# Who forms the low halves of the expert weights in two routing stages: VectorE around each pair of row tiles, in place of GpSimd

## What is computed

```python
x = L0_attn_hidden_states
x = x + 0.5 * _L0_ffn_ref(_layernorm(x), W_gate, b_gate, W_e, b_e)
x = x + _L0_attn_ref(_layernorm(x), Wqkv, q_ln_w, q_ln_b, k_ln_w, k_ln_b, Wout)
x = x + 0.5 * _L0_ffn_ref(_layernorm(x), W_gate, b_gate, W_e, b_e)

def _L0_ffn_ref(x, W_gate, b_gate, W_e, b_e):
    logits = x @ W_gate + b_gate
    _, top_idx = jax.lax.top_k(logits, 2)
    y_all = relu(einsum('bsd,edh->bseh', x, W_e) + b_e)
    return take_along_axis(y_all, top_idx[..., None], axis=2).mean(axis=2)
```

## Time and profile before

| | before |
|---|---|
| median of 3 runs (range) | 1069.3 us (1067.76 to 1070.01) |
| profiled execution: its time, its span | 1067.34 us, 1065.6 us |
| busy: PE, DVE, ACT, POOL | 876.0, 670.0, 443.9, 355.4 us |
| routing 1, up to its last list of tokens | 0 to about 105 us of the span |
| routing 2 | about 784 to 912 us of the span |

### The profile page before, as it was taken

One profiled execution on the slowest core, in us unless ns is written; L12 is line 12 of the kernel. 1 busy time (PEld: TensorE's weight loads), 2 busy tenths in 40 slices (PEclk: granted clock), 3 DMA queues, 4 the chain that ended last, 5 costly groups with the idle time before them and its releaser, 6 DMA issues. The chain is left out here.

```text
span 1065.6 us, 20204 instructions
## 1 busy us (share of the span) xinstructions
PE 876.0 (82%) x6688; PEld 640.8 (60%) x6689; DVE 670.0 (63%) x1295; ACT 443.9 (42%) x817; POOL 355.4 (33%) x340
## 2 busy tenths in 40 slices
PE   3676799993699987838999999999959984699994
PEld 3564688872477776725555555555437863488873
DVE  7977244431788988837777777777527676344431
ACT  3332233331134433334777777777723430133331
POOL 5540677764012321220000000000014440477764
PEclk9997799997799999977999999999979895699997
DMA  8873578863226488664666666554047882378773
GB/s 262 284 261 119 163 143 150 149 120 62 46 85 188 149 217 203 164 201 119 146 147 136 135 138 138 132 137 119 25 134 245 291 277 99 75 141 158 145 134 49
DMA packets 123099, 162.08 MB, mean 152 GB/s; under 512 B 16864, under 2 KB 74336, under 8 KB 122752
## 3 DMA queue, kind: packets, MB, share of 16 engines
q1 hardware_dynamic: 105168, 123.85, 41.5%
q0 software_dynamic: 17856, 37.25, 18.8%
HBM read 97.44 MB, written 67.37 MB: 155 GB/s over the span
## 5 line engine op out<-in xcount | busy, mean ns | idle before, releaser
L825 DVE TENSOR_REDUCE att_part<-att_s_ps 128x2 f32<-128x1024 f32 (+2 forms) x160 | 195.5, 1225 | 67.4 <-PE att_s_ps L673 67.0
L787 ACT ACTIVATE att_prob<-att_st_ps 128x512 f32<-128x512 f32 x320 | 173.7, 595 | 78.4 <-PE att_st_ps L699 78.0
L143 PE MATMUL exp_z_ps<-ex_w_hi,exp_xT_hi 128*128 x312 | 132.7, 425 | 3.4 <-issue 2.1
L144 PE MATMUL exp_z_ps<-ex_w_lo,exp_xT_hi 128*128 x312 | 126.0, 404 | 0.0
L145 PE MATMUL exp_z_ps<-ex_w_hi,exp_xT_lo 128*128 x312 | 125.7, 403 | 0.0
L1459 DVE TENSOR_TENSOR exp_xT_lo<-exp_t_ps,exp_xT_hi 128x512 fp32r<-128x512 f32 x78 | 54.0, 692 | 109.3 <-ACT exp_xT_hi L1445 109.3
L1452 ACT ACTIVATE exp_y<-exp_y 128x512 f32<-128x512 f32 x72 | 45.5, 632 | 170.5 <-DVE exp_y L1471 170.5
L1387 POOL DMA_INDIRECT exp_xg<-xn,ex_token_of x78 | 77.9, 999 | 89.5 <-SPq L1359 61.4
L1094 POOL TENSOR_TENSOR ex_w_lo<-ex_bias,ex_w_hi 128x1024 fp32r<-128x1024 f32 x32 | 75.8, 2368 | 90.0 <-ACT ex_w_hi L1198 89.9
L712 PE MATMUL att_pv_ps<-att_prob,att_v_sb 128*32 128x256 f32 (+2 forms) x1280 | 101.4, 391 | 1.8 <-ACT att_oT L792 1.8
L637 POOL CAST att_m_parts<-att_part 128x28 fp32r<-128x28 f32 x32 | 6.6, 206 | 271.5 <-DVE att_part L829 271.5
(11 more groups left out here) (198 smaller groups left out, 1725.1 us busy)
## 6 DMA issues: line engine op xcount, KB each, us to landing
ex_bias<-in_L_ffn_W_e SPq DMA_DIRECT2D x32, 512.0 KB, 6.5
v_vals<-qkv_vals SPq DMA_DIRECT2D x16, 512.0 KB, 2.8
q_parts<-qkv_partq SPq DMA_DIRECT2D x32, 256.0 KB, 3.3
k_parts<-qkv_partk SPq DMA_DIRECT2D x32, 256.0 KB, 3.7
att_v_sb<-v_vals SPq DMA_DIRECT2D x32, 256.0 KB, 3.5
ex_bias<-in_L_attn_hidden_states SPq DMA_DIRECT2D x8, 512.0 KB, 4.1
acc<-ex_bias SPq DMA_DIRECT2D x8, 512.0 KB, 6.5
xn<-route_xn SPq DMA_DIRECT2D x8, 512.0 KB, 4.9
```

What stands on the lines that cost most here:

```text
L143: nc.tensor.matmul(out, x_hi[:, s], w_hi(c), start=(c == 0), stop=False)
L144: nc.tensor.matmul(out, x_hi[:, s], w_lo(c), start=False, stop=False)
L787: nc.scalar.activation(prob[n % 2][:, col:col + 512], st_ps[(e + half) % 3][:, :], ACT.Exp).then_inc(exp_done, 1)
L825: nc.vector.tensor_reduce(out, src, X_AXIS, ALU.max, negate=True).then_inc(red_done, 1)
```

## The change

GpSimd no longer forms the remainders. A new function `weights_rest(n)` does it on VectorE, with the same operands and the same semaphores. For each pair `u` it is called for piece 2u - 1 before the pair's first instruction and for piece 2u behind the pair's last. The remainder of piece 15 stands behind the last step that picks experts. Both routing stages run this code.

```diff
@@ block.gpsimd
-            for n in range(TILES):
-                pool.wait_ge(w_hi_done, n + 1)
-                nc.gpsimd.tensor_tensor(ex.w_lo[:, 2 * n:2 * n + 2, :], w_stage[n % 2][:, :, :],
-                                        ex.w_hi[:, 2 * n:2 * n + 2, :].bitcast(F32), ALU.subtract).then_inc(w_lo_done, 1)
@@ block.vector
+            def weights_rest(n):
+                dve.wait_ge(w_hi_done, n + 1)
+                nc.vector.tensor_tensor(ex.w_lo[:, 2 * n:2 * n + 2, :], w_stage[n % 2][:, :, :],
+                                        ex.w_hi[:, 2 * n:2 * n + 2, :].bitcast(F32), ALU.subtract).then_inc(w_lo_done, 1)
+
             for u in range(PAIRS):
                 p = u % 2
+                if u >= 1:
+                    weights_rest(2 * u - 1)
                 dve.wait_ge(x_loaded[p], 16 * (u // 2 + 1))
@@
                 for k in range(2):
                     nc.vector.tensor_scalar(xn[p][:, k, :], x[p][:, k, :], mv[:, k, 0:1], rstd[:, k:k + 1],
                                             ALU.subtract, ALU.mult).then_inc(xn_done, 1)
-
+                weights_rest(2 * u)
@@
             nc.vector.tensor_tensor(pair[:, :, 1, :], picked[:, :, :], pair[:, :, 0, :], ALU.subtract).then_inc(picked_done, 1)
+            weights_rest(TILES - 1)
```

## The result

The changed kernel takes 1083.46 us (median of 4 runs, 1081.38 to 1084.26) against 1069.19 us before (4 runs). The ratio on record is 1.0143, 95% interval 1.0118 to 1.0169; the quotient of the two medians is 1.0133. Between the medians the change is slower by 14.3 us, where +13.7 was forecast; by the ratio it is 15.3 us (12.6 to 18.1). The profiled execution has a span of 1079.7 us, against 1065.6.

What follows compares the result with a forecast made beforehand. Routing 1 was taken as paced by SyncE's loop through the store, routing 2 as nearest bound by PE. Terms -3.6 + 7.1 + 10.1 = +13.6 us on 1069.3 gave 1083 us, range 1071 to 1094.

Steps and rivals of the forecast that it cites:

- The subtraction: Both routing stages: one remainder on VectorE takes 1.23 us, bounds 1.15 and 1.3, against 2.37 on GpSimd.
- The tail of routing 1: After the picking, the ranking waits for the second q, k, v piece, delayed by the last remainder: +7.1 us.
- The pairs of routing 1, -3.6 us: Routing 1: without stalls a pair takes 8.7 us instead of 9.2; last xn at 70.5 us against 74.1.
- the loop through the store: SyncE's queue, routing 1: next rows load only once the store of x has landed; 9.2 us a pair, said to stay.
- five transfers at 288 GB/s need 9.1 us; only a fuller queue gives less: Routing 1: five transfers of 512 KB a pair must still pass, limiting how short a pair gets.
- The pairs of routing 2, +10.1 us: Routing 2: a loop through remainder, load, rounding, split and xn makes a pair 12.4 us, against 10.4.
- L: Routing 2: time from load to landing of an even piece, taken as 4.5 us; a pair is 7.9 us plus this.
- the sign of being wrong that the prediction named: Routing 2: ScalarE's split still waiting for PE would show the prediction wrong.
- the covered loop: Rival, routing 2: the loop is covered and the pace stays at 10.4 us a pair; 1071.3 us, chance 0.13.
- the faster VectorE: Rival: routing 1 falls to 7.5 us a pair, routing 2's loop is covered; 1064.1 us, chance 0.06.
- The long loads: Rival, routing 2: loads take 6.5 us, or PE falls to its lower clock; 1095 us, chance 0.13.
- The cancellation: Rival: routing 1 pairs at 8.0 to 8.3 us, routing 2 covered; 1068 to 1071 us, chance 0.04.

Runs made afterwards that it cites:

- last_early: The changed kernel with the last remainder moved from behind the picking of experts to ahead of the logits; 1.0103 of the kernel before.
- w_first: On last_early, SyncE issues the load of the odd piece ahead of the rows and the store of xn in routing 1; 1.0054 of the kernel before.
- r2_only: VectorE forms the remainders in routing 2 alone, GpSimd in routing 1; 1.0062 of the kernel before.
- both_fixed: last_early and w_first together, plus routing 2's even remainder ahead of the second o_rest; 0.9941 of the kernel before.
- the cut ahead of the fork: On last_early, VectorE forms routing 2's even remainder ahead of the second o_rest; 1.0005 of the kernel before.
- the cut of both branches: On last_early, ScalarE does the second split and both copies ahead of the even rounding in routing 2; 0.9993 of the kernel before.
- the cut of one branch: On last_early, ScalarE does only the second split ahead of the even rounding in routing 2; 1.0137 of the kernel before.

## Why the prediction was right, and where its parts were not

**The subtraction:** 1.23 forecast, 1.219 measured.

**The tail of routing 1:** right in mechanism and size. From the end of the picking to the totals 9.7 us were forecast and 9.4 measured (9.7 from its start). That is 6.9 us more than before, where +7.1 was forecast. last_early gives it back.

**The pairs of routing 1, -3.6 us:** mis-sized, and a loop was missing. Measured are -1.5 us at the last xn and +0.2 at the logits. The step that failed is the 8.7 us a pair, with only "the loop through the store" in it; measured were 9.0. A second loop of the same length holds the changed kernel, that of the odd piece: its load stands third in a burst of four, and the rounding begins 6.7 us after it (issued at 58.65, rounding at 65.35), then 1.1 for the rounding, 1.2 for the remainder. In each pair the next odd load goes out within 0.1 us of the end of that remainder. The loop through the store did stay beside it: SyncE stood 7.4 us for the store of x in five waits. w_first shortened both and came to 8.0 us. The step "five transfers at 288 GB/s need 9.1 us; only a fuller queue gives less" was nearly the right doubt: the queue did get fuller, to 330 GB/s. That the logits gain nothing was not foreseen. In the last pairs the copies stand behind a rounding that ends at 69.93 us, and PE's gate products and turns behind them.

**The pairs of routing 2, +10.1 us:** the mechanism holds. From issue to rounding the even pieces took L = 3.9 to 5.0 us, median 4.1 (4.3 for the piece issued at 834.61 and rounded from 838.91), where 4.5 was taken; (881.45 - 809.24) / 6 = 12.03 us a pair, where 12.4 was forecast. In five of these six pairs the second split follows the rounding at once, and the pair is L + 7.7 us in every one of them, where 7.9 + L was forecast. In the sixth (12.7 us, L = 4.1) the split at 827.89 waited 0.85 us for PE, the sign of being wrong that the prediction named; PE had run at a granted clock of 0.50 from 816 to 822 us. The last pair took 8.7 us and not 10.0, and the first xn came 2.4 us earlier in the stage, not 1.5. So counted from the start of the stage the last xn is 5.8 us later and not 10.1. The logits are 8.2 us later, as the copies wait at the end here too. What the prediction left out is that the loop has a second branch behind the rounding, through the copies and PE's gate products; moving the split alone gave no time back.

**The sum:** +3.5 us in routing 1 was +7.0, +10.1 in routing 2 was +8.2, and the rest of the kernel took 1.1 us less. That the total of 1083 fits within a microsecond is luck: these errors have opposite signs. Without any of it the sign was safe: each stage alone is slower by 6 us.

**The rivals:** the covered loop and the faster VectorE both supposed that routing 2 keeps its pace; r2_only refutes it. The long loads supposed L at 6.5 us, or a lower clock; L was 5.0 at most, and the granted clock of the stretch was 0.90, against 0.92 before. The cancellation needed pairs of 8.0 to 8.3 us in routing 1; those came only with w_first, together with the other edits. The Trainium skill's rule that elementwise work belongs on VectorE (GPSIMD Engine Reference, section 4.1) is borne out for the instruction, 1.219 against 2.37 us. For the kernel it did not hold with the lists as they were, 1.43% slower, and did once they fitted, 0.6% faster in both_fixed.

## What to carry to other kernels

When work moves to another engine, price its place in that engine's list before its duration: here 1.2 us of work instead of 2.4 cost 14 us, because it freed a buffer some 4 us later in one stage and let the last buffer go 9 us later in the other. Look for whoever waits for the buffer, and for everything that stands behind that engine's wait; here the cut ahead of the fork and the cut of both branches gave 10 and 12 us back, the cut of one branch none. And a stall that is removed is a gain only once the next loop, which here was only a few tenths of a microsecond shorter, has been shortened too.

## What was not expected

- Blocks that no run changed differ from execution to execution: from the totals of routing 1 to the start of routing 2 it was 692.2 to 699.0 us over 14 profiled executions. What causes it stays open. A stage is compared better by its own start and end than by the span.
- GpSimd's subtraction held up VectorE only in some steps. In the kernel before, GpSimd subtracts from 12.15 to 14.49 us, and VectorE's timeline reads:

```profile
11.51 1.41 DVE L1246 BATCH_NORM_STATS2 route_stats<-ex_bias 128x6 f32<-128x512 f32 x2
12.96 0.40 DVE L1262 BATCH_NORM_AGGREGATE route_mv<-route_stats 128x2 f32<-128x6 f32 x2
13.39 1.12 DVE L80 TENSOR_SCALAR route_tmp_b<-route_mv 128x2 f32<-128x2 f32 x1
```

The statistics take their usual time beside it, and the first small arithmetic step waits until GpSimd is through. In the pairs of routing 1 VectorE's busy time fell by 11.1 us, though 17 us of subtractions were added to it.
